# A decoder kernel on one core: GpSimd's work in the first cross attention moved ahead, three splits sent earlier, MoE's side loads in smaller pieces

## The reference: what is computed

```python
x = LN(x + L0_attn(x))                 # attention on squared distances
x = LN(x + L0_xattn(x, ctx_512))       # 16 heads: causal self attention + cross attention, then @ Wp + bp
x = LN(x + L0_ffn(x))                  # MoE: 8 experts, top 2, each h = silu(x W1 + b1) * (x W2 + b2), h W3 + b3
x = LN(x + L1_attn(x))                 # linear recurrence with complex gates
x = LN(x + L1_xattn(x, ctx_512, ctx_512))
x = LN(x + L1_ffn(x))                  # ternary weights, four products
```

## Time and profile before

| | |
|---|---|
| time of 3 runs | 671.0, 668.37, 666.0 us; median 668.37 |
| profiled execution | 673.8 us, span of its instructions 672.0 us |
| mean granted TensorE clock | 0.963 of full speed |
| busy over the span | PE 91%, DVE 76%, ACT 67%, PEld 51%, POOL 33% |
| first block | to about 381 us |
| MoE block | PE from 386.15 to about 480 us |

### The profile page before, as it was taken

How to read it: one execution, slowest core, us unless ns; L and a number is a source line. 1 busy time by engine, 2 the same in 40 slices (tenths; PEclk the granted TensorE clock), 3 DMA queues, 4 the chain that set the end, 5 groups by cost and what they waited for, 6 DMA issues and landing times. The chain is left out here.

```text
span 672.0 us, 13625 instructions
## 1 busy us (share of the span) xinstructions
PE 613.4 (91%) x5208; PEld 339.5 (51%) x5210; DVE 514.0 (76%) x704; ACT 449.2 (67%) x818; POOL 220.3 (33%) x299
## 2 busy tenths in 40 slices
PE   8979998999999989999999689899719899999996
PEld 5644543444444434444433367688304556657884
DVE  5358996999999989999970349799589767786632
ACT  3555586999999979999999345455782156666224
POOL 8214433243644557767668203000000000014000
PEclk9999997999999999999999969899968999999999
DMA  8257596656656554445411036884000010000000
GB/s 215 96 150 227 180 269 151 151 145 165 156 122 168 132 136 93 94 87 117 101 46 40 17 96 219 315 316 158 1 0 0 5 43 1 2 1 0 1 0 32
DMA packets 44799, 71.39 MB, mean 106 GB/s; under 512 B 13252, under 2 KB 32764, under 8 KB 44352
## 3 DMA queue, kind: packets, MB, share of 16 engines
q1 hardware_dynamic: 31840, 38.34, 21.8%
q0 software_dynamic: 12288, 29.95, 14.6%
q10 hardware_dynamic: 608, 2.25, 1.5%
HBM read 44.94 MB, written 24.81 MB: 104 GB/s over the span
## 5 line engine op out<-in xcount | busy, mean ns | idle before, releaser
L1000 ACT ACTIVATE prob<-ps 128x512 f32<-128x512 f32 (+2 forms) x480 | 251.0, 583 | 30.8 <-PE ps L767 22.8
L1124 DVE TENSOR_REDUCE pm<-ps 128x2 f32<-128x1024 f32 x192 | 224.3, 1209 | 8.6 <-PE ps L725 8.4
L767 PE MATMUL ps<-qq,kc 50*128 50x256 bf16 (+1 forms) x832 | 134.3, 276 | 5.6 <-DMA qq<-mrow 5.6
L790 PE MATMUL ps<-prob,vst 128*9 128x256 f32 (+1 forms) x1664 | 132.2, 383 | 2.8 <-ACT o_all L988 2.8
L725 PE MATMUL ps<-kc,qq 48*128 48x512 bf16 x384 | 118.8, 389 | 1.9 <-DVE pm L1124 1.2
L767 PEld LDWEIGHTS ps<-qq,kc 50*128 50x128 bf16 (+1 forms) x832 | 52.9, 96 | 102.6 <-ACT prob L1000 80.8
L790 PEld LDWEIGHTS ps<-prob,vst 128*9 128x9 f32 (+1 forms) x1664 | 27.7, 88 | 44.4 <-ACT prob L1000 28.4
L713 PE MATMUL ps<-masks_b 64*128 64x256 bf16 x256 | 38.3, 271 | 0.0
L725 PEld LDWEIGHTS ps<-kc,qq 48*128 48x128 bf16 x384 | 34.1, 94 | 8.2 <-DVE pm L1124 3.6
L1460 ACT ACTIVATE sg<-ps,exp_bias 128x512 f32<-128x512 f32 x32 | 21.9, 685 | 21.9 <-PE ps L1376 21.9
L1131 DVE TENSOR_REDUCE nm<-ps 128x4 f32<-128x512 f32 (+1 forms) x32 | 30.6, 957 | 7.6 <-PE ps L713 6.4
(11 more groups left out here) (367 smaller groups left out, 1293.2 us busy)
## 6 DMA issues: line engine op xcount, KB each, us to landing
kc<-kc_scr SPq DMA_DIRECT2D x32, 300.2 KB, 4.8
below<-rden_scr POOLq DMA_DIRECT2D x15, 256.0 KB, 5.9
comb_bc<-comb_scr SPq DMA_DIRECT2D x7, 512.0 KB, 4.4
ctx<-ctx_scr POOLq DMA_DIRECT2D x4, 801.0 KB, 6.6
raw<-in_wexp POOLq DMA_DIRECT2D x8, 384.0 KB, 3.6
exp_scr<-raw_high POOLq DMA_DIRECT2D x8, 384.0 KB, 2.7
exp_scr<-raw_low POOLq DMA_DIRECT2D x8, 384.0 KB, 3.8
kc_scr<-hi SPq DMA_DIRECT2D x6, 400.2 KB, 4.0
```

Of the source, the lines that this page charges most:

```text
L767: last = pe.matmul(bank[0:p, j * TQ:(j + 1) * TQ], kc[s][rows, j, t * 128:t * 128 + p], qq[s][rows, 0, j, :], start=(j == 0), stop=True, s ...
L790: last = pe.matmul(o_ps[32 * hh:32 * hh + VW, kind * TQ + q0:(kind + 1) * TQ], value[:, hh * VW:(hh + 1) * VW], prob[0:k, (NST * n + t) % ...
L1000: act.activation(prob[0:p, g % P_RING, 2 * e:2 * e + 2, q0:TQ], s2[0:p, k % S2_RING, 0:2 * w].rearrange("p (i q) -> p i q", i=2), ACT.Exp, ...
L1124: dve.tensor_reduce(pm[:, m % 2, c, :, jt], banks, AX.X, ALU.max).then_inc(s1_read, 1)
```

## The change: what it does

1. **GpSimd, first block.** An expert's raw load is issued one step ahead of its split (`load_expert`). GpSimd no longer has a part in units 14 and 15: `POOL_UNITS = GATHERED = NU - 2`. Unit 14's sums are spread by PE during the last unit (at its tile 2; the batch projections that stood at tiles 2 and 4 move to 4 and 6), and DVE normalises units 14 and 15 alone, now with one multiplication over 512 columns instead of one over 256.
2. **SP, first block.** Batch 1's parts, kinds "qc", "qs", "ks", go out around the keys of batches 1 and 2 instead of behind `load_unit(2)` and `load_unit(3)`.
3. **MoE.** `ctx_k`, `h1w` and `h2w` are loaded in halves, `ctx_2` in single pieces; a piece is issued with every second tile from the same starting point.

```diff
-            POOL_UNITS = NU - 1
-            GATHERED = POOL_UNITS - 1
+            POOL_UNITS = GATHERED = NU - 2
...
-                    later_splits = {0: [("qc", 1), ("qs", 1)], 1: [("ks", 1)]}
-                    later_splits.update({2 + 3 * b + i: [(kind, 2 + b)] for b in range(2) for i, kind in enumerate(X_KINDS)})
+                    later_splits = {2 + 3 * b + i: [(kind, 2 + b)] for b in range(2) for i, kind in enumerate(X_KINDS)}
                     load_unit(1)
-                    for b in KEYS_BY_SP:
-                        keys_out(b)
+                    for kind, b in zip(X_KINDS, (*KEYS_BY_SP, None)):
+                        split_out(kind, 1)
+                        if b is not None:
+                            keys_out(b)
...
+                    def load_expert(e):
+                        pool.dma_start(raw[e % 2][:], a["wexp"][e, :, 0:3 * DFF]).then_inc(raw_in, 16)
+
                     def split_expert(e):
                         r = e % 2
                         if e >= 2:
                             pool.wait_ge(parts_left[r], 32 * (e // 2))
-                        pool.dma_start(raw[r][:], a["wexp"][e, :, 0:3 * DFF]).then_inc(raw_in, 16)
                         pool.wait_ge(raw_in, 16 * (e + 1))
...
+                    load_expert(0)
                     split_expert(0)
+                    load_expert(1)
                     for n in range(NU - 3):
...
                             split_expert(n + 1)
+                            if n + 2 < E:
+                                load_expert(n + 2)
...
                     normalise(NU - 4)
-                    denominators_out(NU - 2)
                     gather(NU - 4)
                     normalise(NU - 3)
-                    reciprocals_out(NU - 2)
                     gather(NU - 3)
-                    reciprocals_back(NU - 2)
-                    normalise(NU - 2)
-                    pool.wait_ge(last_scaled, 1)
-                    pool.tensor_tensor(o_all[:, NU - 1, 0:TQ], o_all[:, NU - 1, 0:TQ], last_bc[:, 0:TQ], ALU.mult).then_inc(ys, 1)
...
                             if t == 2:
                                 pe.wait_ge(mrow_ready, NU)
                                 pe.wait_ge(later_in, 16 * (len(FOR_BLOCK_3) + 1))
+                                denominators(NU - 2)
+                            elif t == 4:
                                 project_batch(0)
-                            elif t == 4:
+                            elif t == 6:
                                 project_batch(1)
...
                     def last_normalise(n):
-                        o = o_all[:, n, :]
+                        i, o = n - POOL_UNITS, o_all[:, n, :]
                         for kind in range(2):
-                            dve.wait_ge(last_bc_ps, kind + 1)
+                            dve.wait_ge(last_bc_ps, 2 * i + kind + 1)
                             dve.reciprocal(last_bc[:, kind * TQ:(kind + 1) * TQ], ps[:, 6 + kind, 0:TQ]).then_inc(last_scaled, 1)
-                        dve.wait_ge(last_scaled, 2)
-                        dve.tensor_tensor(o[:, TQ:2 * TQ], o[:, TQ:2 * TQ], last_bc[:, TQ:2 * TQ], ALU.mult).then_inc(last_scaled, 1)
-                        dve.wait_ge(last_scaled, 3)
-                        dve.wait_ge(ys, NU)
+                        dve.wait_ge(last_scaled, 3 * i + 2)
+                        dve.tensor_tensor(o, o, last_bc, ALU.mult).then_inc(last_scaled, 1)
+                        dve.wait_ge(last_scaled, 3 * i + 3)
...
-                pool.wait_ge(w3_done, H_FREE + NT)
-                pool.dma_start(later["ctx_k"][:], a["ctx_k"]).then_inc(later_in, 16)
-                for b in range(NB):
-                    if b % 2 == 0:
-                        pool.wait_ge(w3_done, H_FREE + (2 + b // 2) * NT)
-                    pool.dma_start(ctx_2[:, b, :].bitcast(F32),
-                                   ctx_scr[:, :, b, :].rearrange("part p n -> (part p) n")).then_inc(later_in, 16)
-                for i, (n, weight) in enumerate(in_context.items()):
-                    pool.wait_ge(w3_done, H_FREE + (4 + i) * NT)
-                    pool.dma_start(weight, a[n]).then_inc(later_in, 16)
+                half_k = later["ctx_k"].shape[1] // 2
+                halves = [(later["ctx_k"][:, i * half_k:(i + 1) * half_k], a["ctx_k"][:, i * half_k:(i + 1) * half_k]) for i in range(2)]
+                halves += [(ctx_2[:, b, :].bitcast(F32), ctx_scr[:, :, b, :].rearrange("part p n -> (part p) n")) for b in range(NB)]
+                for n, weight in in_context.items():
+                    halves += [(weight[:, i:i + NM // 2], a[n][:, i:i + NM // 2]) for i in range(0, NM, NM // 2)]
+                for i, (dst, src) in enumerate(halves):
+                    pool.wait_ge(w3_done, H_FREE + NT + 2 * i)
+                    pool.dma_start(dst, src).then_inc(later_in, 16)
```

More of the change, by code:

```diff
@@ L858, in denominators @@
                         for kind in range(2):
-                            pe.wait_ge(o_copied, n + kind + 1)
+                            pe.wait_ge(o_copied, n + 1 + (kind if n == NU - 1 else 0))
+                            if n == NU - 1:
+                                pe.wait_ge(last_scaled, kind + 1)
                             pe.matmul(ps[:, 6 + kind, 0:TQ], later["spread"][:], o_all[:, n, kind * TQ:(kind + 1) * TQ],
@@ L1184, in _ @@
                     reciprocals(NU - 3)
+                    last_normalise(NU - 2)
                     projected(0)
-                    reciprocals(NU - 2)
                     last_normalise(NU - 1)
@@ L1326, in _ @@
                         pool.dma_start(later[n][:], a[n]).then_inc(later_in, 16)
-                pool.wait_ge(w3_done, H_FREE + NT)
-                pool.dma_start(later["ctx_k"][:], a["ctx_k"]).then_inc(later_in, 16)
-                for b in range(NB):
-                    if b % 2 == 0:
-                        pool.wait_ge(w3_done, H_FREE + (2 + b // 2) * NT)
-                    pool.dma_start(ctx_2[:, b, :].bitcast(F32),
-                                   ctx_scr[:, :, b, :].rearrange("part p n -> (part p) n")).then_inc(later_in, 16)
-                for i, (n, weight) in enumerate(in_context.items()):
-                    pool.wait_ge(w3_done, H_FREE + (4 + i) * NT)
-                    pool.dma_start(weight, a[n]).then_inc(later_in, 16)
-                pool.wait_ge(later_in, 16 * (len(LATER) + NB + len(in_context)))
+                half_k = later["ctx_k"].shape[1] // 2
[6 more added lines that the diff above has]
+                    pool.dma_start(dst, src).then_inc(later_in, 16)
+                pool.wait_ge(later_in, 16 * (len(LATER) - 1 + 2 + NB + 2 * len(in_context)))
             @block.tensor
@@ L1433, in _ @@
                 pe_ln2(1)
-                pe.wait_ge(later_in, 16 * (len(LATER) + NB + len(in_context)))
+                pe.wait_ge(later_in, 16 * (len(LATER) - 1 + 2 + NB + 2 * len(in_context)))
                 pe.wait_ge(x_ready, 1)
```

## The result

The changed kernel takes 697.68 us (median of 4 runs, 694.65 to 702.5) against 669.68 us for the kernel before, timed beside it: ratio 1.041, 95% interval 1.036 to 1.046. **It is slower by 28 us; 660.0 was forecast.** The profiled execution took 694.65 us, its span is 692.9 us, 20.9 more than before, with a mean granted clock of 0.954.

The account below looks back on a forecast made before the run. PE, 91% busy, was taken to lose time at four waits for late transfers or POOL. 4.8 - 0.8 + 3.5 + 0.6 + 3.2 = 11.3 us off the profiled 673.8 gave 662.5; for the median 660 was forecast, range 654 to 668.

Parts of the forecast that it names:

- Unit 9's maxima rows: First block: with the load a step ahead, PE's 2.33 us wait ahead of unit 9 goes, 3.5 us gained.
- The slower rival: First block: POOL in step bursts onto the maxima rows in five units, 3.5 us each, 677.5 us; chance 0.06.
- Splits at the front: First block's start: 18 added transfers delay SP's first maxima rows, 0.8 us lost, bounds 0 and 7.5.
- Theory S: Front, experiments' theory: SP's own queue costs; two splits fit in two_front (664 to 668), one in one_front (655 to 659).
- Unit 1's wait: First block: SP sends unit 1's maxima rows 2.4 us earlier; the 2.68 us wait and half clock go, 4.8 us gained.
- The block's end: First block's end: PE's 0.61 us wait for POOL's normalisation of unit 14 goes, 0.6 us gained.
- MoE, 3.2 us gained: MoE: with side loads in halves, expert 3's biases land nearly in time, 3.2 us gained, bounds 0 and 4.3.
- Its first rival: MoE: the wait for expert 3's biases stays, same bytes and same queue, 663.2 us; chance 0.18.

Follow-up runs that it names:

- tail_back: tail_only with the read-back of the reciprocals asked for before the next expert's split, without the load ahead: 657.08 us, ratio 0.986.
- back_first: The changed kernel with GpSimd's broadcast read-back of the reciprocals asked for before the next expert's split: 676.36 us, ratio 1.017.
- repaired: The changed kernel with the read-back before the next expert's split and only the "qc" split at the front: 668.30 us, ratio 0.999.
- apart_2: repaired with the load ahead issued behind the step's first send, which waits for ACT's copy: 659.39 us, ratio 0.986.
- load_start: The changed kernel with the load ahead put before `denominators_out`, in effect sent one place behind the read-back: 691.86 us, ratio 1.039.
- split_only: The kernel before with only batch 1's three splits moved to the front: 679.61 us, ratio 1.013.
- two_front: The kernel before with two of the second batch's splits, qc and qs, sent at the front: 671.01 us, ratio 1.007.
- one_front: tail_back with split qc sent at the front, qs after unit 0's maxima rows and ks after unit 1's: 656.23 us, ratio 0.982.
- tail_only: The kernel before with only the first block's end changed, units 14 and 15 normalised by DVE: 662.88 us, ratio 0.988.
- tail_late: tail_only with GpSimd allowed to leave the block only after DVE's first reciprocal of unit 15: 670.53 us, ratio 1.001.
- moe_only: The kernel before with only the MoE's side loads in smaller pieces: 671.21 us, ratio 0.999.
- moe_later: The kernel before with `ctx_k` asked for NT tiles later in the MoE: 675.69 us, ratio 1.006.

## Why the prediction was wrong

1. **Unit 9's maxima rows, taken at 3.5 us gained: the step that failed.** Its own text had the other end, 17.5 us lost in units 4 to 8, and chose against it because only one of sixteen sends had been late. That counted places instead of asking what in the old order had kept them apart. The 28.1 us that POOL waited for its raw loads lay between each load and its writes and made POOL's steps longer than a unit, so that its writes drifted along the unit instead of meeting SP's sends each time: in the kernel before they go out 3.2 and 7.6 us behind the rows of units 4 and 5, and 5.3, 3.4 and 2.5 us ahead of those of units 7, 8 and 9, and only the last of these stalls PE. In tail_back a load is followed by 4.9 us of waiting on average, with SP's sends in it in the step shown. The change took these waits for waste. Without them two writes, a load and the read-back leave POOL in 2.4 us, and the first write goes out within 1 us of SP's sends in units 4 to 8 (in unit 8 there is no load left, and PE still waits 2.54 us). The prediction's counterargument, that POOL had been in step before without harm, rested on few meetings; unit 3's is the one close to SP's sends. Nor was unit 9's wait one that only some executions have: all seven traced kernels with the old order of load and read-back have it, 1.29 to 2.78 us. The measured price is 22.0 us in the profiled execution, where 3.5 were to be gained, and by the runs 2.4% for the read-back (changed kernel to back_first) and 1.3% more for the load (repaired to apart_2).
2. **The slower rival** (chance 0.06) is what came to pass, in its mechanism, its units and its number of stalls. Its price of 3.5 us each was too small: the copies of units 2 and 9 are 148.16 us apart, 25.5 more than seven pitches, in place of 17.5, since a stall of 4.5 us costs 6.2 with the clock. The forecast's other gains that it started from were mostly not there.
3. **Splits at the front, taken at 0.8 us lost, bounds 0 and 7.5.** It was 8.9. The reckoning took the splits' pace from SP's queue with only its own loads around it. Three cost 15.9 us rather than 12.1, and behind them the four small sends were slow to issue and to land, which the step did not price. That part varies: in load_start, with the same front, it is absent, and PE begins 4.7 us late. Against 0.8 both are large; 8.9 is beyond the upper bound too. Theory S's small remedy, one split early, has none of it.
4. **Unit 1's wait, 4.8 us gained**: gone in the changed kernel, split_only, two_front and one_front. The size was about right: in one_front the first block ends 4.4 us earlier than in tail_back. That only 0.8 us of it reach the median is another matter (above).
5. **The block's end, 0.6 us gained.** The price was 3.4 to 3.75 us up to the MoE's first product and the cause another: not PE's 0.61 us for unit 14, but POOL's late leaving of the block, which the next block's first product waits for. tail_only and tail_late show it. The row was there before, 5.39 us of PE's idling ahead of 386.15, and the prediction passed it over as if it belonged to every change of block.
6. **MoE, 3.2 us gained.** Its first rival was right: same bytes, same wait. The step reckoned that ever shorter packets let the biases pass; moe_only (ratio 0.999, the wait at 1.97 us) and moe_later show that what POOL has asked for ahead of them decides.

The Trainium skill ("DMA: Bandwidth & Descriptors", section "Queues, rings and completion order") has an engine drain a whole packet of one queue before it turns to another. By that rule a small send can be held behind a large one's packets. The trace agrees as to the outcome, 4.52 us of wait for 8 KB sent amid 1.4 MB. Whether the grain is its packet of several descriptors or a single transfer's piece no run here shows.

## What to carry to other kernels

A wait on an engine off the critical path may be the spacing of a shared queue: before it is removed, write down which transfers then leave together, and which small transfer of another queue must land in that time. Send large loads after the small, waited-for ones (as in apart_2), not as early as possible. Look at the change of block on its own, since here the engine that left last set it, though its work was not waited for.

## What was not expected of the hardware

- The next block's first product came 8.7 us after GpSimd's last instruction of the block had ended (376.73 + 0.73 to 386.15) in the kernel before, though DVE's last add had ended 4.6 us before that product. With GpSimd's last send 18 us ahead of that add, in the changed kernel, only 1.3 us of idling are left. In tail_late GpSimd may leave once the first of two reciprocals has ended (two from 375.11 in 3.37 us, so at about 376.8), and the product comes 8.7 us behind that too, by this estimate.
- A broadcast read-back of 256 KB over 128 partitions had the DMA engines at a mean busy share of 0.26 and 98 GB/s; in the burst it took 10.2 us from issue to landing (4.9 us with the queue nearly its own). Moving it ahead of the split, 5 us earlier, was worth 2.4% of the kernel (20.6 us between the profiled spans).
- Issuing can be slowed too: in four of the five profiled kernels with all 18 split transfers at the front SP took 5.20 to 6.53 us for four sends of 2 KB, in the fifth (load_start) 2.88 us, as without them. What decides this is open.
- The MoE block, from its first product to its end, took 91.3 us in tail_back, 94.5 in one_front and 97.5 in tail_only, with the same instructions. Differences of this size between single profiled executions say nothing about the first block.
